# Attention over 16 graphs on one core: the mask's turn goes from TensorE to transposing DMAs and GpSimd, k3's stack is sent in three parts, two bo sums move

## The reference

```python
h = jnp.maximum(_layernorm(x, axis=-1), 0.0)           # x: (16, 512, 512)
q, k, v = heads(h @ Wq + bq), heads(h @ Wk + bk), heads(h @ Wv + bv)
scores = jnp.einsum('bhqd,bhkd->bhqk', q, k) * scale
scores = jnp.where(adj[:, None] == 0, -jnp.inf, scores)
attn = jax.nn.softmax(scores, axis=-1)
out = jnp.einsum('bhqk,bhkd->bhqd', attn, v)
return x + (out.transpose(0, 2, 1, 3).reshape(b, s, 512) @ Wo + bo)
```

## Time and profile before

| | |
|---|---|
| median of 3 runs | 1655.04 us (1654.94 to 1660.1) |
| the profiled execution | 1660.24 us, its span 1658.4 us |
| TensorE busy | 1602.3 us (97%) |
| ScalarE busy | 1455.7 us (88%) |
| VectorE busy | 1438.9 us (87%) |
| GpSimd busy | 710.7 us (43%) |
| TensorE's granted clock | 0.987 of full over the span |

### The profile page before, as it was taken

One profiled execution on the slowest core, in us unless ns is written; L12 is line 12 of the kernel. 1 busy time (PEld: TensorE's weight loads), 2 busy tenths in 40 slices (PEclk: granted clock), 3 DMA queues, 4 the chain that ended last, 5 costly groups with the idle time before them and its releaser, 6 DMA issues.

```text
span 1658.4 us, 27600 instructions
## 1 busy us (share of the span) xinstructions
PE 1602.3 (97%) x7745; PEld 1032.7 (62%) x7745; DVE 1438.9 (87%) x3504; ACT 1455.7 (88%) x3500; POOL 710.7 (43%) x641
## 2 busy tenths in 40 slices
PE   6799999999999999999999999999999999999997
PEld 5556666666666666666666666666666666666643
DVE  5889889898889989889898889889889898888885
ACT  3699899998999989899989989998999988989984
POOL 2044444443443544443543543544443543543442
PEclk9799999999999999999999999999999999999998
DMA  6434343433434344343434434344343434433320
GB/s 209 103 92 114 96 117 89 120 94 115 122 89 119 91 121 112 96 121 85 125 94 115 123 83 124 90 121 109 97 122 85 125 92 115 122 79 104 93 74 26
DMA packets 117167, 175.17 MB, mean 106 GB/s; under 512 B 30860, under 2 KB 32920, under 8 KB 117016
## 3 DMA queue, kind: packets, MB, share of 16 engines
q1 hardware_dynamic: 112536, 171.83, 38.1%
q10 hardware_dynamic: 4480, 1.58, 0.4%
HBM read 54.79 MB, written 16.78 MB: 43 GB/s over the span
## 4 chain that ended last, share of the span: by engine, by line
PE 80%; DVE 9%; ACT 5%; issue 4%; SPq 1%; DMA 1%; DVEq 0%; ACTq 0%
PE psP L757 36%; PE ps L821 15%; PE psO L851 13%; PE ps L833 12%; ACT ps L444 3%; DVE ps L608 2%; DVE probs L622 2%; PE ps L771 2%; PE ps L777 1%; DVE stats L521 1%; DVE part_lo L663 1%; ACT probs L484 1%; DVE neg_max L608 1%; DVE probs L625 1%; ACT bias_k L501 1%
## 5 line engine op out<-in xcount | busy, mean ns | idle before, releaser
L359 POOL TENSOR_TENSOR probs<-probs,keep_k 128x512 int32<-128x512 int32 x438 | 570.2, 1322 | 717.9 <-ACT probs L484 716.0
L608 DVE CUSTOM_DVE_ANT_0 ps<-ps,bias_q 128x512 f32<-128x512 f32 x1024 | 706.7, 691 | 170.8 <-PE ps L821 165.3
L444 ACT ACTIVATE ps<-ps,neg_max 128x512 f32<-128x512 f32 x1024 | 686.3, 670 | 111.9 <-DVE neg_max L608 88.4
L484 ACT ACTIVATE probs<-ps 128x512 f32<-128x512 f32 x1024 | 617.9, 604 | 17.0 <-PE ps L833 14.7
L821 PE MATMUL ps<-k_stack,q_stack 96*128 96x512 f32 x1024 | 451.8, 442 | 30.2 <-ACT ps L444 23.8
L833 PE MATMUL ps<-q_stack,k_stack 98*128 98x512 f32 x1024 | 411.6, 403 | 4.2 <-ACT probs L484 3.8
L821 PEld LDWEIGHTS ps<-k_stack,q_stack 96*128 96x128 f32 x1024 | 193.2, 189 | 291.3 <-ACT ps L444 196.2
L622 DVE SCALAR_TENSOR_TENSOR probs<-bias_k,probs 128x512 f32<-128x512 bf16 x512 | 361.7, 707 | 3.3 <-ACT probs L484 3.2
L851 PE MATMUL psO<-probs,v_sb 128*32 128x512 f32 x2048 | 276.2, 611 | 5.1 <-ACT probs L484 2.3
L833 PEld LDWEIGHTS ps<-q_stack,k_stack 98*128 98x128 f32 x1024 | 195.6, 191 | 45.1 <-ACT probs L484 18.6
L444 ACT ACTIVATION_READ_ACCUMULATOR ps<-ps,neg_max 128x1 f32 x1024 | 215.8, 211 | 0.0
(11 more groups left out here) (79 smaller groups left out, 1928.5 us busy)
## 6 DMA issues: line engine op xcount, KB each, us to landing
q_stack<-part_hi SPq DMA_DIRECT2D x512, 64.0 KB, 2.0
k_stack<-part_hi SPq DMA_DIRECT2D x504, 64.0 KB, 2.0
x_tile<-in_x_dram SPq DMA_DIRECT2D x66, 256.0 KB, 3.0
adj_tile<-in_adj_dram SPq DMA_DIRECT2D x64, 256.0 KB, 3.1
q_stack<-part_lo SPq DMA_DIRECT2D x256, 64.0 KB, 2.0
k_stack<-part_lo SPq DMA_DIRECT2D x256, 64.0 KB, 2.0
y_tile<-in_x_dram SPq DMA_DIRECT2D x62, 256.0 KB, 2.9
out_dram<-y_tile SPq DMA_DIRECT2D x62, 256.0 KB, 2.1
```

Source lines behind the costliest of these rows:

```text
L359: nc.gpsimd.tensor_tensor(bits, bits, keep_k[:, kt // 2, :], ALU.mult).then_inc(gpsimd_masked, 1)
L444: nc.scalar.activation(item, item, ACT.Exp, scale=-1.0, bias=neg_max[:, g % 2, col:col + 1], accum_out=exp_sum[:, col:col + 1]).then_inc(e ...
L484: nc.scalar.activation(probs[:, n % P_RING, :], ps2[:, n % 2, :], ACT.Exp, scale=SCALE).then_inc(exp2_done, 1)
L608: nc.vector.tensor_tensor_reduce(bank1(k, ("s", u)), bank1(k, ("s", u)), bias_q[:, qt, :], -SCALE, 3.0e38, ALU.add, ALU.min, neg_max[:, g ...
```

## The change

- The m turns leave `TURNS`, and with them TensorE's transposes and ScalarE's two copies. `turn_mask` has SyncE issue four transposing DMAs a half, at slot 49 (half 0) and slot 58 (half 1), each 128 x 256 bfloat16 of `bias_q` into two key tiles of a new tile `turned`.
- `turned[:, 0:2]` is `bias_k`. `turned[:, 2:4]` holds the key tiles for `keep_k`; the same bytes serve as `adj_tile` at other times, so `load_adj` waits for `keep_done` too.
- GpSimd widens `turned[:, 2 + half]` into `keep_k` (`form_keep`), at slots 55 and 62.
- k3's stack is sent in three parts of four DMAs at slots 8, 10 and 12, not in slot 1.
- `add_bo` for tiles 2 and 3 goes from slots 8 and 12 to slots 10 and 15.

```diff
-TURNS = {1: [("h", 0, 0)], 3: [("m", 1, -1)], 5: [("h", 1, 0)], 8: [("c", 1, -1)], 10: [("h", 2, 0)], 13: [("h", 3, 0)],
-         24: [("c", 2, -1)], 40: [("c", 3, -1)], 53: [("m", 0, 0)], 56: [("c", 0, 0)]}
+TURNS = {1: [("h", 0, 0)], 5: [("h", 1, 0)], 8: [("c", 1, -1)], 10: [("h", 2, 0)], 13: [("h", 3, 0)],
+         24: [("c", 2, -1)], 40: [("c", 3, -1)], 56: [("c", 0, 0)]}
-        adj_tile = sb("adj_tile", [P, S], I32)
+        turned = sb("turned", [P, NT, S], BF16)
+        bias_k = turned[:, 0:2, :]
+        adj_tile = turned[:, 2:4, :].rearrange("p a s -> p (a s)").bitcast(I32)
-        bias_k = sb("bias_k", [P, NT // 2, S], BF16)
                     sp.wait_ge(bias_done, due(4 * b + t))
+                    sp.wait_ge(keep_done, due(2 * b))
+            def turn_mask(b, half):
+                if have(b):
+                    sp.wait_ge(bias_done, 4 * b + 4)
+                    sp.wait_ge(keep_done, due(2 * b - 1 + half))
+                    sp.wait_ge(vector_masked, due(vector_before(64 * (b - 1) + 48 + 8 * half + 4)))
+                    for t in range(NT):
+                        sp.dma_start_transpose(turned[:, half::2, P * t:P * t + P],
+                                               bias_q[:, t, 2 * P * half:2 * P * half + 2 * P]).then_inc(m_in[half], 16)
+                    if u in (49, 58): turn_mask(k, (u - 49) // 9)
+                    if u in (8, 10, 12) and have(k - 1):
+                        load_stack(sp, k - 1, 7, (("hi0",), ("lo",), ("hi1",))[(u - 8) // 2])
-                    if u % 4 == 1:
-                        done = tile_at(k, u // 4 - 1) if u >= 4 else tile_at(k - 1, 15)
+                    if u % 4 == 1 and u > 1:
+                        done = tile_at(k, u // 4 - 1)
+            def form_keep(b, half):
+                if have(b):
+                    pool.wait_ge(m_in[half], 64 * (b + 1))
+                    pool.wait_ge(vector_masked, due(vector_before(64 * (b - 1) + 48 + 8 * half + 8)))
+                    pool.wait_ge(gpsimd_masked, due(gpsimd_before(64 * (b - 1) + 48 + 8 * half + 8)))
+                    nc.gpsimd.tensor_scalar(keep_k[:, half, :], turned[:, 2 + half, :], -1.0 / MASKED, 1.0, ALU.mult, ALU.add
+                                            ).then_inc(keep_done, 1)
+                    if u in (55, 62): form_keep(k, (u - 55) // 7)
-                    if u == 8 and k - 2 != LAST: add_bo(k - 2, 2)
-                    if u == 12 and k - 2 != LAST: add_bo(k - 2, 3)
+                    if u == 10 and k - 2 != LAST: add_bo(k - 2, 2)
+                    if u == 15 and k - 2 != LAST: add_bo(k - 2, 3)
-                        if kind == "m" and have(k + rel):
...
-                            nc.scalar.activation(bias_k[:, n, :], turned[:, 0:S], ACT.Identity).then_inc(bias_k_done, 1)
...
-                            nc.scalar.activation(keep_k[:, n, :], turned[:, S:2 * S], ACT.Identity,
-                                                 scale=-1.0 / MASKED, bias=1.0).then_inc(m_done, 1)
-                    dve.wait_ge(m_turned, due(2 * b))
+                    dve.wait_ge(m_in[0], due(64 * b))
+                    dve.wait_ge(m_in[1], due(64 * b))
-                            dve.wait_ge(bias_k_done, due(2 * b + kt // 2 + 1))
+                            dve.wait_ge(m_in[kt // 2], due(64 * (b + 1)))
-                            dve.wait_ge(m_done, due(2 * b + kt // 2 + 1))
+                            dve.wait_ge(keep_done, due(2 * b + kt // 2 + 1))
-                elif kind == "m":
-                    pe.wait_ge(bias_done, due(4 * b + 4))
-                    for i in range(2 * NT):
-                        key_tile, t = 2 * n + i // NT, i % NT
-                        last = nc.tensor.transpose(bank[:, 64 * i:64 * i + 64].bitcast(BF16),
-                                                   bias_q[:, t, P * key_tile:P * key_tile + P], ident_b)
-                    last.then_inc(m_turned, 1)
```

More of the change, by code:

```diff
@@ L140, in attention_block @@
         bias_done = sem("bias_done")
-        m_turned, bias_k_done, m_done = sem("m_turned"), sem("bias_k_done"), sem("m_done")
+        m_in, keep_done = [sem("m_in0"), sem("m_in1")], sem("keep_done")
         qkv_done, out_done = sem("qkv_done"), sem("out_done")
@@ L261, in load_adj @@
                     sp.wait_ge(bias_done, due(4 * b + t))
-                    sp.dma_start(adj_tile[:], adj_rows[bass.ds(row, 1)].rearrange("a p d -> (a p) d")
+                    sp.wait_ge(keep_done, due(2 * b))
+                    sp.dma_start(adj_tile, adj_rows[bass.ds(row, 1)].rearrange("a p d -> (a p) d")
                                  ).then_inc(adj_in, 16)
+            def turn_mask(b, half):
[6 more added lines that the diff above has]
+                                               bias_q[:, t, 2 * P * half:2 * P * half + 2 * P]).then_inc(m_in[half], 16)
             def load_y(b, t):
@@ L355, in mask @@
                 if n < 16 and n % 4 == 0:
-                    pool.wait_ge(m_done, due(2 * b + kt // 2 + 1))
+                    pool.wait_ge(keep_done, due(2 * b + kt // 2 + 1))
                 pool.wait_ge(exp2_done, due(64 * b + n + 1))
@@ L495, in step @@
                                                  ACT.Relu).then_inc(h_hi_done, 1)
-                        if kind == "m" and have(k + rel):
-                            b = k + rel
-                            act.wait_ge(m_turned, due(2 * b + n + 1))
-                            turned = bank1(k, (kind, n, rel)).bitcast(BF16)
-                            act.wait_ge(vector_masked, due(vector_before(64 * (b - 1) + 48 + 8 * n + 8)))
-                            nc.scalar.activation(bias_k[:, n, :], turned[:, 0:S], ACT.Identity).then_inc(bias_k_done, 1)
-                            act.wait_ge(gpsimd_masked, due(gpsimd_before(64 * (b - 1) + 48 + 8 * n + 8)))
-                            nc.scalar.activation(keep_k[:, n, :], turned[:, S:2 * S], ACT.Identity,
-                                                 scale=-1.0 / MASKED, bias=1.0).then_inc(m_done, 1)
             blocks(step, first=0)
@@ L534, in form_bias @@
                 if have(b):
-                    dve.wait_ge(m_turned, due(2 * b))
+                    dve.wait_ge(m_in[0], due(64 * b))
+                    dve.wait_ge(m_in[1], due(64 * b))
                     dve.wait_ge(masked_max, due(64 * (b - 1) + 48 + 4 * t + 4))
                     dve.wait_ge(adj_in, due(16 * (4 * b + t + 1)))
-                    nc.vector.tensor_scalar(bias_q[:, t, :], adj_tile[:], 0.0, MASKED, ALU.is_equal, ALU.mult
+                    nc.vector.tensor_scalar(bias_q[:, t, :], adj_tile, 0.0, MASKED, ALU.is_equal, ALU.mult
                                             ).then_inc(bias_done, 1)
@@ L712, in wait_bank1 @@
                         pe.wait_ge(h_lo_done, due(4 * b + n + 1))
-                    elif kind == "m":
-                        pe.wait_ge(m_done, due(2 * b + n + 1))
                     else:
```

## The result

The kernel after takes 1644.28 us (median of 6 runs, 1642.73 to 1649.14), the kernel before took 1655.74 beside it (6 runs, 1653.86 to 1661.23): ratio 0.9932, 95% interval 0.9915 to 0.9948, faster by 11.5 us. The forecast was 12.2 us less, 1642.8. The profiled executions lie further apart, 1660.24 and 1643.36: 16.9 us. One of the six runs of experiment 8 took 2412.9 us, at a granted clock of 0.581 where the others had 0.984 to 0.988; its ratio leaves that run out.

What follows compares the result with a forecast made beforehand. TensorE, busy 97%, was taken as the bound, so only work leaving it or its waits could pay. 18.2 + 5.5 - 3.0 - 1.6 - 6.9 = 12.2 us saved, giving 1642.8 us; range 1630 to 1676.

Steps and rivals of the forecast that it cites:

- Half 1: Mask turn in slot 3, slots 2 to 6: 1.14 us a block saved, 18.2 us in 16 blocks.
- Half 0: Mask turn in slot 53, slots 50 to 58: 0.37 us a block saved, 5.5 us in 15 blocks.
- GpSimd's form: GpSimd's new mask-forming operations: 0.9 us each, holding VectorE's two-input operations, 3.0 plus 1.6 us lost.
- The transposing DMAs: Eight a block on SyncE's queue: cost nothing while the mask's halves land before GpSimd wants them.
- rival C: Queue too slow: half 1 lands late, GpSimd's masks and slot 6's sum wait; 1685 at X = 2.49; chance 0.21.
- X: SyncE queue time of one transposing DMA: taken as 1.0 us, between 0.62 and 2.49.
- k3's stack and the bo sums: Tile 3's sum starts just before VectorE's multiply of slot 13: 0.6 us lost in each of 14 blocks, 6.9 net.
- half 0 with its locks: Slot 53's saving of 5.5 us less 3.0 us for GpSimd's form holding VectorE, 0.2 a block.
- half 1's form: GpSimd's form in slots 61 to 64 delays VectorE: 0.1 us a block, 1.6 us in 16 blocks.
- A: Rival: GpSimd's operations miss VectorE's multiplies and tile 3's sum keeps its distance; 23.7 us saved, 1631; chance 0.12.
- B: Rival: GpSimd's form takes 1.3 us and meets a multiply each time, eating the gain; 1655 to 1668; chance 0.16.
- D: Rival: the mask's turn was hidden anyway, so nothing is gained; 1655; chance 0.01.

Runs made afterwards that it cites:

- experiment 8: Kernel after with tile 3's statistics, root and normalise later and tile 1's bo sum moved from slot 54 to 4: 1633.14 us, ratio 0.9846 to before.
- Experiment 3: Kernel after with half 0 turned on TensorE and copied by ScalarE as before: 1643.42 us, ratio 0.9915 to before.
- experiment 10: Kernel after with half 0 turned on TensorE and tile 1's bo sum in slot 4 instead of 54: 1639.92 us, ratio 0.9904 to before.
- experiment 7: Kernel after with tile 1's bo sum moved from slot 54 to slot 4 of the next block: 1632.6 us, ratio 0.9842 to before.
- experiment 11: Kernel before with only tile 1's bo sum moved from slot 54 to slot 4: 1656.28 us, ratio 0.9994 to before.
- Experiment 6: Kernel after with tile 3's statistics, root and normalise in slots 59, 60, 63 instead of 55, 56, 60: 1643.95 us, ratio 0.9906 to before.
- Experiment 4: Kernel after with ScalarE forming keep_k in slots 56 and 63, instead of GpSimd in 55 and 62: 1656.25 us, ratio 0.9994 to before.
- experiment 5: Kernel after with half 1's four transposing DMAs issued at slot 62 instead of 58: 1766.58 us, ratio 1.065 to before.
- experiment 9: Kernel after with each transposing DMA cut into two of 128 x 128, eight a half: 1758.09 us, ratio 1.0607 to before.
- experiment 1: Kernel before with k3's stack in three parts and two bo sums moved, the mask's turn left on TensorE and ScalarE: 1656.19 us, ratio 1.0.
- experiment 2: Kernel after with k3's stack whole in slot 1 and the bo sums in slots 8 and 12, as before: 1672.61 us, ratio 1.01 to before.

## Why the prediction came out as it did

**Half 1 (right, and by its mechanism).** 1.14 us a block were forecast, slots 3 and 4 gave 1.18; 16 blocks make 18.9 against 18.2. Experiment 3 shows that this is the whole gain of the change. That VectorE could follow is seen in the window: 5.40 us of work in 6.50.

**Half 0 (the place right, the size wrong).** The step took 0.37 us a block for the turn and 0.2 off for locks. In slots 53 to 55 it is 0.52 and 0.39 gained and 0.63 lost, 0.28 net. But slot 1 takes 0.25 more, and experiment 3, which keeps half 0 on TensorE, doesn't show it there (1.89): half 0's change causes it. Net 0.03 us a block, and 0.9915 against 0.9932 in the runs. The step said that VectorE gives back only part because its list has no gap. It missed what in that list could be moved. The bo sum of tile 1 holds a multiply for 0.96 us. Before, the turn's wait ran in the same time. Slots 53 to 55 last 5.51 us with both (before), 5.51 with the turn alone (experiment 10), 5.22 with the sum alone (after) and 4.56 with neither (experiment 7). In the runs each removal alone gives nothing (the kernel after against that of experiment 3; experiment 11 against before, and 10 against 3), and both together give 0.9842 against 0.9915: 12 us.

**Slot 1 (not foreseen).** The timelines of after:

```profile
758.57 5.38 POOL L374 TENSOR_TENSOR probs<-probs,keep_k 128x512 int32<-128x512 int32 x4
...
762.86 1.38 DVE L545 TENSOR_SCALAR x_tile<-x_tile,mean_var,rstd 128x512 f32<-128x512 f32 x1
```

GpSimd's fourth mask ends at 763.95, and VectorE's normalise, 0.54 us alone, ends at 764.24. At this place before:

```profile
763.26 5.39 POOL L359 TENSOR_TENSOR probs<-probs,keep_k 128x512 int32<-128x512 int32 x4
...
767.80 1.14 DVE L529 TENSOR_SCALAR x_tile<-x_tile,mean_var,rstd 128x512 f32<-128x512 f32 x1
```

In each of the blocks 2 to 14 of both kernels the normalise ends 0.28 or 0.29 us behind the end of a mask. It starts 0.35 to 0.51 us behind the start of that mask before and 0.18 to 0.34 after: half 0's saving has shifted VectorE's list against GpSimd's masks. The normalise takes 1.36 us in the mean, 1.12 before, and slot 1 is 0.74 to 0.80 us longer than it in each block of both. The prediction let only two-input operations be held, so it had no price for this one. Experiment 6 takes the normalise away from the masks, and slot 1 goes back to 1.89.
The Trainium skill ("SBUF — State Buffer", section on the two separate sides) names both kinds for VectorE's side of the shared port pair: two inputs in SBUF, or a mode that uses two ports. The trace agrees in so far as the one-input normalise is held, 1.38 us beside 0.54; in which mode it runs, no trace here shows. The prediction had weighed only the first kind.

**GpSimd's form (smaller than taken).** It costs 0.70 us, not 0.9, and it does hold VectorE: 1.10 us for a multiply that starts 0.05 behind a form, 0.69 alone (rows of experiment 7). The multiplies above 0.8 us beside a form are six in the whole run, 1.5 us in all, against 4.6 forecast. Experiment 4 shows what the copy would have cost on ScalarE: all of the gain.
The same section of the Trainium skill lets any GpSimd operation hold the pair, with one input too; the 1.10 us agree, and no row of before could have shown it.

**The transposing DMAs (rival C's chain borne out, its price too low).** X is 1.25 us, in the range of 0.62 to 2.49, below the 2.15 from which C decides, and half 1 lands in time. No run stands near 2.15: a half in eight DMAs (10.08 us) is like X = 2.5, and there it decides. Experiments 5 and 9 put it past the point, one by a later issue, one by more DMAs: the chain that C names is there in each, in that order. C's price left out the clock's fall: 5.37 us of standstill cost 7.5 in slots 6 and 7 in experiment 5, 3.89 cost 6.1 in experiment 9.
The page "DMA: Bandwidth & Descriptors" of the Trainium skill (latency and other measured facts) gives a bandwidth, and so 0.25 us for 64 KB, an estimate. The queue's time is five times that and hardly depends on the bytes (1.246 and 1.232 us), so bandwidth isn't what a transposing DMA of this size is priced by.

**k3's stack and the bo sums (wrong).** The step that failed is "I take 0.6 us in each of 14 blocks", 6.9 us in all, and under it the place of the meeting, load_y "some 0.7 us later". The price of one meeting was right: in experiment 1 the one sum that starts 0.06 us ahead makes the multiply 1.77 us long. The queue of after:

```profile
780.89 3.36 SPq L234 DMA_DIRECT2D k_stack<-part_hi  x4
784.29 0.89 SPq L292 DMA_DIRECT2D out_dram<-y_tile  x1
...
787.74 0.58 SPq L285 DMA_DIRECT2D y_tile<-in_x_dram  x1
```

and what GpSimd and VectorE do with it (answers to the earlier trace rows):

```profile
789.67 0.69 DVE L639 SCALAR_TENSOR_TENSOR probs<-turned,probs 128x512 f32<-128x512 bf16 x1
...
790.64 1.28 POOL L365 TENSOR_TENSOR y_tile<-y_tile,bo_row 128x512 f32<-128x512 f32 x1 [1.29 <-DMA y_tile<-in_x_dram]
...
791.50 0.96 DVE L639 SCALAR_TENSOR_TENSOR probs<-turned,probs 128x512 f32<-128x512 bf16 x1
```

The first part of the stack takes 3.36 us, not 2.5, and in this block y comes so late that the sum starts 0.97 us behind the multiply of slot 13 and 0.86 ahead of the next one, which takes 0.96 us and not 0.69. Over blocks 2 to 15 the sum starts 0.08 to 1.11 us behind the multiply of slot 13, where it started 0.8 ahead in most blocks before. In nine blocks it is 0.08 to 0.51 behind, and the multiplies take 0.69; in the other five the next one takes 0.73 to 1.10; in none is it 0.1 to 0.3 ahead. Slot 15 lasts 1.38 or 1.39 us in all of them. A meeting was priced as if its place were known within 0.2 us, but it is spread over 1 us. Slots 15 and 18 together are even 0.17 shorter after than before. Before, slot 15 is long in blocks 2, 4 and 14 (2.04, 1.83 and 1.60 us), where the sum met the multiply; the prediction counted two of these three. In other kernels the two slots last from 3.10 (experiment 1) to 3.23 (experiment 7), so a difference of this size comes with the profiled execution, and I don't count it to the change. And the step's sign missed the main thing. The part isn't a cost of the change but its condition (experiment 2, which doesn't separate the stack from the sums). The prediction had worked out that the transposing DMAs push the stack back, but only asked whether the stack's own readers would wait, and not who waits behind it in the queue.

**The sum.** Forecast by terms: 18.2, 2.5 (half 0 with its locks), -1.6, -6.9. Measured in slots: 18.9, 4.2, -4.0 (slot 1), 2.5 (slots 15 and 18), and -2.4 in slots 27 and 39, which no step had. That is 19.2 against 16.9 between the profiled executions, and 11.5 between the medians. Against the forecast slots 15 and 18 came out 9.4 us better and the two halves 2.4; slot 1 came out 2.4 worse than the 1.6 for half 1's form, and slots 27 and 39 took another 2.4. The forecast meets the median within 1.5 us by luck, then: errors of both signs stand in it, and the two profiled executions lie 5.4 us further apart than the medians. Slot 27's 0.07 is one block, in which TensorE waited 0.78 us for a DMA of c's row (2.33 us, 1.39 or 1.40 in the other 13). Why slot 39 is longer by 0.07 in nearly every block, and by 0.42 in one, stays open.

**The rivals.** A (no collisions, 1631) and B (locks eat the gain) were each half true: what GpSimd holds costs slot 55 and slot 1 all that half 0 gave, and slot 15 nothing. But what holds there is a bo sum and the masks, which GpSimd had before, not B's form: in experiment 4, without it, slot 55 stays at 2.15 us and the normalise at 1.35. D is excluded for half 1. For half 0 its time came true and its reason didn't: slots 53 and 54 gave 0.91 us a block, so the turn wasn't hidden; slots 55 and 1 took it back.

## What to carry to other kernels

When two waits end at the same place, removing one gives nothing and the other is then the bound: follow the list of the engine that waits next back to its first operation that is longer than usual, and move what held it in the same change. When a queue gets more work, price what stands behind it, not only what it carries: here 10 us of transposing DMAs a block, with the stack whole, made y late, GpSimd's masks late and TensorE wait, until the stack was cut up and moved and the sum of tile 2 stood behind two of the masks. And don't price a collision at a place that is worked out from a queue's times to less than a few tenths of a us; keep both signs.

## What the runs showed of the hardware

- A transposing DMA on SyncE's queue takes 1.25 us of it for 128 x 256 bfloat16 and 1.23 for 128 x 128; a plain one of 64 KB takes 0.59 (medians). From issue to landing it is 2.4 us, a plain one's 2.0.
- GpSimd's one-input operation over 128x512, bfloat16 to int32, takes 0.62 us alone, where a two-input one on int32 takes 1.32.
- VectorE's normalise (one input, float32) is held by a GpSimd mask as a two-input operation is: 1.38 us, not 0.54. GpSimd is held in turn when VectorE starts first: 1.75 us, not 1.3, for a sum that starts 0.08 us behind a multiply. VectorE can still pay behind it: an operation of 128x16 took 1.27 us, not 0.17, beside such a sum.
- Behind a standstill of 4.80 us TensorE ran at a granted clock of 0.51 for 5.1 us.
